# A convolution-attention-experts kernel on one Trainium2 core: body loop turned by a stage, half of the experts moved to the second attention, layer norm row quantities on quarters

## The reference

```python
xn = group_norm(x)                           # 32 groups
x  = x + proj(attention(qkv(xn)))            # 8 heads of 32, full 1024x1024 weights
t  = to_tokens(x)
t  = t + W_O(attention(QKV(_ln_t(t))))       # 8 heads, masked
xt = _ln_t(t)
sel = sigmoid(xt @ expert_sel.T)             # 32 experts, the best 2 of each token
h   = relu(einsum('td,edh->teh', xt, keys))  # 64 wide each
t   = t + einsum('teh,te,ehv->tv', h, w, values)
```

## Time and profile before

| | us |
|---|---|
| median of 3 runs | 3855.47 (3851.91 to 3858.39) |
| the profiled execution's own time | 3846.6 |
| its span, first to last instruction | 3844.9 |

### The profile page before, as it was taken

One profiled execution on the slowest core, in us unless ns is written; L12 is line 12 of the kernel. 1 busy time (PEld: TensorE's weight loads), 2 busy tenths in 40 slices (PEclk: granted clock), 3 DMA queues, 4 the chain that ended last, 5 costly groups with the idle time before them and its releaser, 6 DMA issues.

```text
span 3844.9 us, 54190 instructions
## 1 busy us (share of the span) xinstructions
PE 3322.6 (86%) x17874; PEld 1820.9 (47%) x17874; DVE 2186.7 (57%) x2905; ACT 1670.4 (43%) x2604; POOL 425.7 (11%) x539
## 2 busy tenths in 40 slices
PE   5898799987998879988799788997889988899779
PEld 2344464435644356344563445534465344554347
DVE  6634585356843568445674447744567355773544
ACT  1454335533364333644236342463424634355333
POOL 0000030001300013000230002200022000320005
PEclk7798899988999889989899888998979989899889
DMA  3011340114402144021530205302142021421125
GB/s 99 1 45 34 90 137 28 45 34 110 139 7 52 26 123 126 11 57 26 140 106 17 61 18 140 99 17 61 29 138 88 18 61 43 143 70 34 45 57 165
DMA packets 151942, 263.02 MB, mean 68 GB/s; under 512 B 26832, under 2 KB 28880, under 8 KB 151504
## 3 DMA queue, kind: packets, MB, share of 16 engines
q1 hardware_dynamic: 151632, 259.15, 24.8%
HBM read 145.80 MB, written 9.44 MB: 40 GB/s over the span
## 4 chain that ended last, share of the span: by engine, by line
PE 61%; issue 14%; DVE 12%; ACT 7%; SPq 3%; DMA 2%; POOL 1%; DVEq 0%; ACTq 0%; POOLq 0%
PE ps_acc L592 8%; PE ps_two L705 7%; PE ps_one L544 7%; DVE tops L1072 6%; PE ps_two L669 6%; PE ps_acc L604 6%; PE ps_one L546 5%; PE ps_one L545 5%; PE ps_acc L544 3%; PE ps_acc L545 3%; PE ps_acc L546 3%; PE ps_one L705 3%; ACT probs L879 2%; SPq L457 2%; PE ps_two L686 1%
## 5 line engine op out<-in xcount | busy, mean ns | idle before, releaser
L1072 DVE TENSOR_REDUCE tops<-ps_two 128x2 bf16<-128x1024 f32 (+3 forms) x896 | 964.0, 1112 | 415.0 <-PE ps_two L669 247.2
L879 ACT ACTIVATE probs<-ps_two 128x1024 f32<-128x1024 f32 (+1 forms) x704 | 641.6, 961 | 234.4 <-PE ps_two L705 151.6
L669 PE MATMUL ps_two<-stacks 32*128 32x512 f32 (+3 forms) x1792 | 425.1, 506 | 178.0 <-DVE tops L1072 141.8
L705 PE MATMUL ps_two<-stacks 97*128 97x512 f32 (+3 forms) x1408 | 472.9, 442 | 67.8 <-ACT probs L879 37.7
L592 PE MATMUL ps_acc<-probs,v_sb 128*32 128x512 f32 (+3 forms) x3584 | 459.7, 587 | 0.0
L519 POOL TENSOR_TENSOR nat<-expert_sb,nat 128x256 fp32r<-128x256 f32 x512 | 386.3, 756 | 654.8 <-ACT nat L819 557.1
L705 PEld LDWEIGHTS ps_two<-stacks 97*128 97x128 f32 x1408 | 243.3, 196 | 357.4 <-ACT probs L879 184.7
L669 PEld LDWEIGHTS ps_two<-stacks 32*128 32x128 f32 x1792 | 171.5, 202 | 453.7 <-DVE tops L1072 237.0
L819 ACT CAST nat<-expert_sb 128x256 fp32r<-128x256 f32 x256 | 103.4, 407 | 630.3 <-DVE probs L1181 519.6
L604 PE MATMUL ps_acc<-probs,ones 128*32 128x512 f32 (+3 forms) x2944 | 358.4, 560 | 0.0
L525 POOL TENSOR_TENSOR act_lo<-xn,act_hi 128x2048 fp32r<-128x2048 f32 x8 | 36.1, 4511 | 2757.0 <-ACT act_hi L929 2757.0
(11 more groups left out here) (131 smaller groups left out, 4504.6 us busy)
## 6 DMA issues: line engine op xcount, KB each, us to landing
stacks<-nat SPq DMA_DIRECT2D x792, 128.0 KB, 2.4
expert_sb<-experts_dram SPq DMA_DIRECT2D x256, 256.0 KB, 2.8
probs<-gates_dram SPq DMA_DIRECT2D x512, 128.0 KB, 3.0
x_in<-x_in_dram SPq DMA_DIRECT2D x9, 1024.0 KB, 4.9
out_dram<-x_res SPq DMA_DIRECT2D x16, 512.0 KB, 2.9
probs<-mats_dram SPq DMA_DIRECT2D x1, 2048.0 KB, 9.3
gates_dram<-w_turn SPq DMA_DIRECT2D x64, 16.0 KB, 1.6
sel_w<-sel_dram SPq DMA_DIRECT2D x1, 32.0 KB, 8.4
```

Of the source, the lines that this page charges most:

```text
L669: mm = pe.matmul(acc[:, HALF * e:HALF * e + n_keys], q_st[rows, g, j, P * i:P * i + P], k_st[rows, g, j, HALF * kh:HALF * kh + n_keys], st ...
L705: mm = pe.matmul(at[:, a:HALF], k_st[0:MID + 1, g, j, P * k:P * k + P], q_st[0:MID + 1, g, j, HALF * hf + a:HALF * hf + HALF], start=True, ...
L879: done(act.activation(probs[:, n % 2, per * i:per * i + per, a:HALF], acc[:, :, a:HALF], ACT.Exp, scale=SCALE), s + (i,))
L1072: done(dve.reduce_max(tops[:, kh, 2 * pr:2 * pr + 2, i], acc[:, :, 0:cols(st, i, kh)], AX_X), s)
```

## The change

The section `body` now begins earlier in the chain of a batch, right after the last mixes of the second attention. The final output, layer norm of the second half, logits and turn of that half now stand between tops and ups of the next iteration. The experts of half 0 stand in the first attention's tops; those of half 1 in the second attention's tops. All mixes are wide and stand in a row. Gates, inputs and turn go by halves. The gates' ring has 2 buffers, `gated` has 2. The low part of the gated h moves from DVE to POOL. Experts' weights are read into `probs`, sums are added up in `xn`. The inputs of half 1 are kept in the place of the first two weight matrices, which are written to DRAM once at the start and read back in each iteration (`reload`); the residual of half 1 is copied by a DMA (`keep`). In layer norm the rows of 512 become four quarters of 32 partitions by 128 columns: 8 matmuls of 128 columns by 32 weights make them, DVE and ACT work on 128x128, and 4 matmuls with `quarter_w` spread them out again, once for the mean and once for the inverse root.

```diff
-    def experts_of(self, tops):
-        ups = [("up", hf, j) for hf in range(self.halves) for j in range(self.experts)]
-        steps = spread(ups, tops) if tops else ups
...
+    def up(self, hf, j):
+        return [("up", hf, j)] + ([("dn", hf, j - 2)] if j > 1 else [])
+    def ups(self, hf, start):
+        out = [s for j in range(start, self.experts) for s in self.up(hf, j)]
+        return out + [("dn", hf, self.experts - 2), ("dn", hf, self.experts - 1)]
     def first(self):
-        return [("stats",), ("gn",), ("split", 0), ("split", 1)] + self.qk(0, 0) + self.v(0)[:2]
+        return [("stats",), ("gn",), ("split", 0)] + self.qk(0, 0, [0])
...
+        t = rows_later(self.first_tops(0) + self.first_tops(1))
+        if later:
+            steps = [("div", 1, 1, 1)] + self.qk(0, 1, [0]) + [("fin", 1, 1, 1)] + self.v(0)[:2] + [("inputs", 0)]
+            steps += t[:2] + self.out(1, 1) + [("fetch", 0)] + t[2:4] + [("split", 1), ("keep",)] + up(0, 0)
+            steps += t[4:6] + [("lna", 1, 1)] + up(0, 1) + [("lnm", 1, 1)] + self.qk(0, 0, [1]) + t[6:8] + [("lnb", 1, 1)] + up(0, 2)
+            steps += [("lnr", 1, 1)] + self.qk(0, 1, [1]) + t[8:10] + up(0, 3) + [("logits", 1)] + self.v(0)[2:] + t[10:12] + up(0, 4)
+            steps += [("inputs", 1)] + t[12:14] + [("turn", 1)] + spread(self.ups(0, 5), t[14:])
...
+        steps += d[:1] + [("norm", 0, 0, 1), d[1]] + self.qk(1, 0, [0]) + [("div", 0, 0, 1), d[2], ("fin", 0, 0, 1)] + d[3:]
+        t, u = rows_later(self.top(1, 0, 0)), rows_later(self.top(1, 1, 0))
+        steps += [("norm", 0, 1, 1), ("div", 0, 1, 1)] + self.qk(1, 1, [0]) + t[:3] + [("fin", 0, 1, 1)] + t[3:5]
+        steps += self.out(0, 1) + ([("fetch", 1)] if later else []) + t[5:8] + up(1, 0) + [("lna", 0, 1)] + t[8:]
+        steps += [("lnm", 0, 1)] + up(1, 1) + u[:3] + [("lnb", 0, 1)] + up(1, 2) + u[3:5] + [("lnr", 0, 1)] + up(1, 3) + u[5:8]
+        steps += [("parts", 1)] + up(1, 4) + u[8:] + self.qk(1, 0, [1]) + up(1, 5) + self.v(1)[:2] + up(1, 6) + self.qk(1, 1, [1]) + up(1, 7) + self.v(1)[2:]
+        t = rows_later(self.top(1, 0, 1) + self.top(1, 1, 1))
+        steps += spread(self.ups(1, 8), t) if later else t
+        e, f, g, h = (self.mix(1, g, hf, True) for hf in (0, 1) for g in (0, 1))
+        steps += e[:1] + ([("down", 1), ("reload",)] if later else []) + e[1:]
...
+        steps += h[:1] + [("norm", 1, 0, 1), h[1], ("logits", 0), h[2], ("div", 1, 0, 1), h[3], ("split", 0), ("fin", 1, 0, 1)]
+        steps += [h[4], ("turn", 0), h[5]] + self.qk(0, 0, [0]) + [h[6], h[7], ("norm", 1, 1, 1)]
...
+    GATES = 2
...
+            sp.dma_start(w_image[0], f(w_hi[:, 0:2, :, :]).rearrange("p m k c -> p (m k c)")).then_inc(imaged, 16)
...
+                    if s[0] == "fetch":
+                        hf = s[1]
...
+                        for j in range(RING):
+                            load_expert(j)
+                        hold(gates_out, "turn", sec.no["turn"][("turn", 1)] if hf else 0, 16 * PH)
+                        for j in range(GATES):
+                            load_gates(hf, j)
                     if s[0] == "up":
...
+                        _, hf, j = s
+                        if 1 <= j and j - 1 + GATES < ET:
+                            read(("up", hf, j - 1))
+                            load_gates(hf, j - 1 + GATES)
+                        if j + RING < ET:
+                            hold(vals_down, "up", sec.no["up"][s])
+                            load_expert(j + RING)
+                    if s[0] == "keep":
+                        read(("out", 1, 1, CT - 1))
+                        hold(acts_lo, "acts", sec.no.get("acts", {}).get(("split", 1), 0))
+                        sp.dma_start(xt[:, :, :], x_res[:, :, half(1)]).then_inc(kept, 16)
+                    if s[0] == "reload":
+                        read(("up", 1, ET - 1))
+                        for both, n in ((w_hi, 0), (w_lo, 1)):
+                            sp.dma_start(f(both[:, 0:2, :, :]).rearrange("p m k c -> p (m k c)"), w_image[n]).then_inc(reloaded, 16)
...
+                        lower(hf, j, vals_up, vals_parts, C, vals_down)
+                        pool.wait_ge(gated_up, sec.value("up", sec.no["up"][s]))
+                        pool.tensor_tensor(gated_lo[:, j % 2, :], gated[:, j % GATES, :], f(gated_hi[:, j % 2, :]),
+                                           ALU.subtract).then_inc(gated_down, 1)
...
+                def by_quarter(acc, columns):
+                    for k in range(CT):
+                        for q in range(PH):
+                            mm = pe.matmul(acc[HD * q:HD * q + HD, 0:P], mean_w[:, 0:HD], columns(k, P * q),
+                                           start=(k == 0), stop=(k == CT - 1))
+                    return mm
+                def spread_out(acc, quarters):
+                    for q in range(PH):
+                        mm = pe.matmul(acc[:, P * q:P * q + P], quarter_w[:, q, :], quarters[:, 0:P], start=True, stop=True)
+                    return mm
...
+                        for g in range(CT):
+                            for j in range(G):
+                                act.wait_ge(stacked[g][0][j], sec.value(f"stacks{g}0", sec.stacks_so_far(s, g, 0), STACK))
+                        for j in range(2):
+                            upper_keys(s[1], j)
...
+                    elif kind == "dn" and s[2] + 2 < ET:
+                        act.wait_ge(downed, sec.value("up", sec.no["up"][("up",) + s[1:]]))
+                        upper_gated(s[2] + 2)
```

More of the change, by code:

```diff
@@ L105, in batch, with first_tops @@
-    def batch(self, experts):
-        tops = rows_later(self.top(0, 0, 0) + self.top(0, 0, 1) + self.top(0, 1, 0) + self.top(0, 1, 1))
-        if experts:
-            steps = self.qk(0, 1, [0]) + [("logits",)] + self.v(0)[2:] + self.qk(0, 1, [1]) + [("inputs",)]
-            steps += tops[:3] + [("turn",)] + tops[3:10] + self.experts_of(tops[10:])
-        else:
-            steps = self.v(0)[2:] + self.qk(0, 1) + tops
+    def first_tops(self, g):
+        per_half, pairs = self.tiles // self.halves, range(HEADS_PER_GROUP // 2)
+        early = [("top", 0, g, pr, i, 0) for pr in pairs for i in range(per_half)]
+        return early + [s for hf in range(self.halves) for s in self.top(0, g, hf) if s not in early]
@@ L180, in events @@
             add("acc", s)
-        if kind in ("split", "parts", "inputs"):
+        if kind == "down":
+            add(f"store{s[1]}", s)
+        if kind in ("split", "parts"):
             add("acts", s)
@@ L232, in value, with stacks_so_far @@
             return n * each
+        def stacks_so_far(self, s, g, hf):
+            return sum(t[0] == "stack" and t[2:] == (g, hf) for t in self.steps[:self.steps.index(s)])
         def any(self, kind, n):
@@ L930, in emit @@
+                        act.copy(late_hi if hf else act_hi[:, :, half(0)], xn[:, :, half(hf)]).then_inc(inputs_hi, 1)
                     elif kind == "turn":
+                        full(s)
+                    elif kind == "fetch":
                         for g in range(CT):
[L933 to L936 removed]
```

373 lines of the change are left out of this document (187 added, 186 removed).

## The result

The changed kernel takes 3911.33 us (median of 4 runs, 3891.49 to 3914.9) against 3856.93 for the kernel before beside it: ratio 1.013, 95% interval 1.011 to 1.016. It is slower, by 1.3%; 3575 was forecast. The profiled execution took 3908.69 us, its span is 3906.4, the mean clock 0.892 (before 0.896).

What follows compares the result with a forecast made beforehand. No engine alone was taken to bound the kernel (last chain 61% PE). Head 390 + 7 x 432 + last 150 + 2 outside the span = 3566, median 9 above: 3575 us; range 3400 to 3800, forecast case 3480 to 3700 (0.58).

Steps and rivals of the forecast that it cites:

- The sign: Whole kernel: chance 0.86 of being faster than before, 0.04 the same, 0.10 slower.
- C: Stage of the first attention's mixes: 103 us an iteration.
- E: Stage of 24 wide mixes closing the second attention: 79 us, with no tops left to fill waits.
- D: Stage of the second attention's tops with 16 ups: 117 us, in parts of 68 and 49.
- of which PE has other work for 7: 5; up 8's gates likewise, 4: Gate loads issued behind a stack in D's first part: 11.7 us latency, mostly covered, leaving waits of 5 and 4.
- A: Stage from body start to turn, with 13 tops and 8 expert halves: 54 us, 40 of it work.
- B: Stage of 51 tops with 11 ups: 79 us, bound by DVE (74) with PE at 60.
- Rival 3: SP's queue exposed, gates and first experts behind stacks: +49 us an iteration, 3923 us, slower than before; chance 0.10.
- Head: Time before the first iteration: 390 us (380 to 412), with D without experts about 72.
- Last: Part after the last iteration: 150 us (135 to 165), ups paced at 3.65 each by the gates' ring of two.
- Layer norm: Quarter products and spreads on PE: 2.8 us (2.2 to 4.5); DVE's small operations 0.3 us each.
- Rival 2: Clock falls in DVE-paced parts, half of B and D at 1.2 GHz: B +10, D +22, 3801 us; chance 0.12.

Runs made afterwards that it cites:

- e1: The changed kernel with the gate rows of expert j+2 issued once VectorE has read the up of expert j: 3801.42 us, ratio 0.984.
- e5: e1 with division and group 1's projection moved to the iteration's end, and the first batch's tops and mixes moved earlier: 3825.58 us, ratio 0.992.
- e9: e1 with a half's two projections kept further apart in the iteration alone, boundary and head as in the changed kernel: 3778.84 us, ratio 0.979.
- e8: e5 with a half's two projections kept further apart and the halves alternating in the first batch: 3778.28 us, ratio 0.979.
- e3: The changed kernel with the low part of the gated product made by VectorE again instead of GpSimd: 3918.42 us, ratio 1.014.
- e12: e10 with each row maximum on VectorE taken over only the first half of its columns, so not the whole work: 3604.20 us, ratio 0.934.
- e2: The changed kernel with layer norm mean and variance back on full rows of 512, without the quarters: 3940.10 us, ratio 1.020.
- e11: e10 with twenty unread filler matmuls before the wait of each half's first up: 3768.40 us, ratio 0.976.
- e10: e8 with group 1's first-half query and key projection of each attention moved ahead of the norm, among the last mixes: 3759.38 us, ratio 0.975.

## Why the prediction was wrong

- **The sign.** What was to be won was about 36 us an iteration by full stages C and E; they are full (PE 97% and 96% in the rows above). The forecast failed in the stages that fill up with the moved chains.
- **D, "of which PE has other work for 7: 5; up 8's gates likewise, 4".** This is the first step that failed, and the largest that a run takes away. The latency of 11.7 us was about right; the cover was not. VectorE stood for 11.36 and 12.18 us where 5 and 4 were counted, since the copies of the projections that TensorE would have worked on are VectorE's too. e1 takes these waits away and D comes to 119.9 against 117: 10.5 of D's miss of 13.4 is this one term. Rival 3 named the place; I gave it 0.10, for want of following who feeds TensorE while VectorE waits. That its 3923 lies 12 us from the measured time is luck: it put 49 us more an iteration on the queue, and e1 finds 12.7.
- **A, "Sum 54".** Measured 64.3. Two things were missing: the jump of the loop inside the division (6.18 us on ScalarE) and `nat`, which holds a half's second projection back until the first one's stacks have landed. The second hid the first: the boundary alone gave nothing (e5), `nat` alone 4.1 us (e9), both 6.4 (e1 to e8). Starting the stacks at the norm gave another 5.4, which C and E paid back. A then stands at 52.8. The change had put these steps behind one another, where the kernel before alternated the halves.
- **B, "DVE bounds ... 79".** Measured 89.3, with VectorE busy 78% of it and not over 90%. Its amount of work was right (70 us, 74 forecast) but was not the bound by itself: e3 gives it 6 us more and B is no longer, e12 takes 24 away and B falls by 15, most of it in TensorE's busy time. The sum prices TensorE's work at full speed, 60 us, and adds 0.2 us for each of its absences; TensorE was in fact busy for 68 to 76 us, as the clock stood at 0.92 to 0.82. A line through those two ends, an estimate from the rows, meets 1.00 at 78 us, the forecast's own number. So the clock goes with nearly the whole miss of B; no run changed it by itself, so that it is the cause stays argued.
- **C 105.9 for 103, E 82.9 for 79.** Small. The quarters account for 0.7 us of E at the same clock, 2.3 with the clock that came with them (e2).
- **Head, 444.5 for 390.** VectorE's first top starts at 73.6 us in place of 57.0, because all four stacks' projections stand ahead of the tops, and D without experts has nothing to put between two projections: it takes 98 us, 72 forecast. e8's order of the head gives back 21 us. **Last: 151.7 for 150**, right for this order of the queue; e1's 134.1 with the same two buffers shows that the ring alone does not set it.
- **Layer norm.** VectorE's small operations take 0.29 us (0.3 forecast). On TensorE, in E of the kernel after:

```profile
2296.76 0.64 PE L679 MATMUL ps_one<-squares,mean_w 128*32 128x128 f32 x16
2302.01 1.15 PE L686 MATMUL ps_one<-rstd,quarter_w 128*128 128x128 f32 x8 [2.05 <-DVE rstd L1227]
```

  Twice 0.64 + 1.15 make 3.6 us for 2.8, inside the bounds. The rule of the Trainium skill (TensorEngine Tiling (Array Packing), Key Properties), that a change of the tiling mode drains TensorE, would by the prediction's sum add 2.8 us to an iteration. E shows 0.7 for one norm at the same clock and C nothing (106.2 with full rows, 105.9 without), so no run here settles it.
- **Rival 2, the clock.** The mean of the whole run is 0.892 for 0.896, so it explains little of the loss against the kernel before. Against the forecast it matters: the rival asked 10 us more for B, and B's miss is 10.3, at a mean clock of 0.86. Its 22 us for D did not come: D, at 0.90, fell to 119.9 with the gates alone. It is thus borne out in B only, and e11 finds no gain behind its two waits.

Of the iteration's 41 us, e1 shows 12.7 and e8 5.8. e10 moves A to its forecast but not the iteration. The rest is mostly B, which goes with the clock and was not taken apart by a run. Moving the stack transfers to a queue that holds no engine up was not tried.

## What to carry to other kernels

When steps are moved past an in-order DMA queue, list for each small load what stands ahead of it and issue it as soon as its buffer is free, not at the step that will use it: one move in the queue was worth 2.8% here. When a wait is said to be covered, name the instruction that covers it and check that it doesn't itself need the engine that waits. A staging tile shared by two producers is a wait that shows only when they come to stand next to each other, so remove suspects together before calling one of them free. Where a hardware loop repeats the same work, compare its iterations: a stage whose length goes with the granted clock while the other engines' busy time stays the same may have been priced at the wrong clock, and the rows say so before any experiment.

## What was unexpected of the hardware

- Two queues issuing the same kind of transfer side by side put twelve of 128 KB out in 4.4 us in place of 7.7, but each then lands after 4.4 us and not 2.4.
- An engine that issues transfers itself loses about what the queue did: six cost ScalarE 4.26 us.
- The loop's jump leaves ScalarE idle for 5.3 to 6.7 us and TensorE for 3.0 to 4.0 with nothing in the profile to hold them.
- Executions of one kernel differ with the clock: e8 took 3750.26 us at a mean of 0.909 and 3788.23 at 0.898. So do the iterations of one execution: B took 84.6 us at 0.92 and 92.8 at 0.82.
